# Expert rows turned by 32x32 blocks on VectorE and regrouped by SBUF transfers, from the eighth group on; last group's weight copies issued by ScalarE

## The reference

```python
H = jax.nn.gelu(xf @ W1 + b1, approximate=False)          # 128 -> 512
probs = jax.nn.softmax((H @ Wg + bg) / TEMP, axis=-1)
assign = jnp.argmax(probs, axis=-1)
for e in range(Wd.shape[0]):                               # 8 experts
    y = H @ Wd[e] + bd[e]                                  # 512 -> 128
    sel = (assign == e)[:, None]
    out = out + jnp.where(sel, probs[:, e:e + 1] * y, 0.0)
```

## Time and profile before

| | us |
|---|---|
| runs, median of 3 | 542.11 |
| lowest, highest | 538.12, 544.45 |
| the profiled execution | 537.82 |
| its span | 536.1 |

### The profile page before, as it was taken

One profiled execution on the slowest core, in us unless ns is written; L12 is line 12 of the kernel. 1 busy time (PEld: TensorE's weight loads), 2 busy tenths in 40 slices (PEclk: granted clock), 3 DMA queues, 4 the chain that ended last, 5 costly groups with the idle time before them and its releaser, 6 DMA issues.

```text
span 536.1 us, 10215 instructions
## 1 busy us (share of the span) xinstructions
PE 485.8 (91%) x3048; PEld 392.9 (73%) x3048; DVE 358.3 (67%) x1151; ACT 318.3 (59%) x572; POOL 363.9 (68%) x352
## 2 busy tenths in 40 slices
PE   8999999999999999999989777977697998997983
PEld 4788888888878888888866545645386986986972
DVE  4788777998879888888789463835554552562532
ACT  3877977688667877878795553825342333333330
POOL 4489976999879988987777754554535462564555
PEclk9999999999999999999998897978788997997998
DMA  7512454112631111111210111113212323432110
GB/s 207 151 56 86 136 168 129 46 53 58 204 94 57 54 50 52 48 49 51 60 45 29 46 45 40 40 61 107 85 34 77 89 81 109 130 121 85 50 40 21
DMA packets 66341, 42.10 MB, mean 79 GB/s; under 512 B 9436, under 2 KB 61920, under 8 KB 66288
## 3 DMA queue, kind: packets, MB, share of 16 engines
q1 hardware_dynamic: 60464, 32.13, 20.8%
q0 software_dynamic: 4224, 8.92, 4.8%
q10 hardware_dynamic: 1600, 0.40, 0.3%
HBM read 16.90 MB, written 9.84 MB: 50 GB/s over the span
## 4 chain that ended last, share of the span: by engine, by line
PE 79%; issue 6%; DVE 5%; ACT 3%; another core or an unknown queue 2%; SPq 2%; DMA 0%; POOL 0%; POOLq 0%; DVEq 0%; ACTq 0%
PE bank L594 17%; PE bank L596 17%; PE bank L595 16%; PE bank L833 12%; PE bank L625 7%; PE bank L760 2%; ACT adj_i L1043 2%; PE bank L809 1%; PE bank L716 1%; PE bank L612 1%; PE bank L632 1%; SPq L358 1%; SPq L362 1%; ACT xn L950 1%
## 5 line engine op out<-in xcount | busy, mean ns | idle before, releaser
L1043 ACT ACTIVATE adj_i<-bank,b1c 128x512 f32<-128x512 f32 x132 | 86.0, 690 | 136.8 <-PE bank L596 75.6
L559 POOL DMA_INDIRECT sorted_rows<-xrow,pos x64 | 61.9, 967 | 54.8 <-issue 54.8
L459 POOL TENSOR_TENSOR diff<-hT,n_sb 128x512 f32<-128x512 f32 x48 | 68.2, 1420 | 16.8 <-ACT n_sb L932 16.7
L833 PE MATMUL bank<-wd_sb,adj_i 128*128 x512 | 65.8, 285 | 7.4 <-issue 6.1
L833 PEld LDWEIGHTS bank<-wd_sb,adj_i 128*128 128x128 f32 x512 | 62.7, 200 | 9.4 <-issue 8.9
L594 PE MATMUL bank<-hT_hi,w_hi 128*128 128x512 f32 x132 | 61.9, 469 | 5.1 <-issue 4.0
L461 POOL TENSOR_TENSOR diff<-z_sb,diff 128x512 f32<-128x512 f32 x48 | 62.5, 1303 | 3.8
L594 PE MATMUL bank<-ag_hi,wf_hi 128*128 128x512 f32 x144 | 58.9, 409 | 0.4 <-DVE ag_lo L1198 0.3
L595 PE MATMUL bank<-hT_lo,w_hi 128*128 128x512 f32 x132 | 56.7, 430 | 2.2 <-issue 2.1
L596 PE MATMUL bank<-hT_hi,w_lo 128*128 128x512 f32 x132 | 56.8, 430 | 0.8 <-issue 0.8
L595 PE MATMUL bank<-ag_lo,wf_hi 128*128 128x512 f32 x144 | 57.0, 396 | 0.0
(11 more groups left out here) (200 smaller groups left out, 1084.8 us busy)
## 6 DMA issues: line engine op xcount, KB each, us to landing
bands<-hT SPq DMA_DIRECT2D x192, 64.0 KB, 2.2
adj_i<-sorted_rows SPq DMA_DIRECT2D x64, 72.0 KB
xrow<-in_x_dram SPq DMA_DIRECT2D x16, 256.0 KB, 3.2
adj_i<-in_adj_dram SPq DMA_DIRECT2D x16, 256.0 KB, 3.6
sorted_rows<-xrow,pos POOLq DMA_INDIRECT x64
A<-wd_sb SPq DMA_DIRECT2D x4, 256.0 KB
hT<-wd_sb SPq DMA_DIRECT2D x4, 256.0 KB
sorted_rows<-padrow SPq DMA_DIRECT2D x9, 72.0 KB
```

What stands on the lines that cost most here:

```text
L459: nc.gpsimd.tensor_tensor(diff[:, b, :], hT[:, g, :], n_sb[:, b, :], ALU.subtract).then_inc(diff_ok, 1)
L559: nc.gpsimd.indirect_dma_start(out=sorted_rows, out_offset=bass.IndirectOffsetOnAxis(ap=pos[:, g, j:j + 1], axis=0), in_=xrow[:, g * GR + ...
L833: last = nc.tensor.matmul(o, HT[:, sg % 2, k, j * P:(j + 1) * P], wd_sb[:, bass.ds(at + k * P, P)], start=(k == 0), stop=(k == KC - 1))
L1043: nc.scalar.activation(HT[:, hb, k, 0:n], HB[k][:, 0:n], ACT.Gelu, bias=b1c[:, k:k + 1]).then_inc(done, 1)
```

## The change

From group 7 on (`BANDED` = `EARLY_SG` + 1), TensorE no longer transposes the rows. VectorE normalises group s+3 in step s (it was s+2) and transposes it by 32x32 blocks into `bands` (`row_blocks`), reading every fourth element. SyncE then issues four SBUF transfers per group (`rows_turned`), which put the blocks together in `hn`, one load of rows later. ScalarE and VectorE read `hn` where they read pT. As the turned rows come in another order of columns, the Gelus undo it: `slot_gelus` reads and writes by runs of 32 elements (up to group 6 both sides are so viewed, in the same order). The copies for the last group, with their sixteen registers, go from SyncE to the end of ScalarE's steps 6 to 14. In step 4 VectorE normalises two groups, 6 and 7.

```diff
--- before.py
+++ after.py
@@ -209,6 +209,7 @@
         e_in, e_xn, e_t, e_xhi, e_xlo, e_w1, e_h, e_y, e_yb, e_yo, e_out = (
             sem("e_" + n) for n in ("in", "xn", "t", "xhi", "xlo", "w1", "h", "y", "yb", "yo", "out"))
         e_home = sem("e_home")
+        e_blk, e_col = sem("e_blk"), [sem("e_col"), sem("e_col_odd")]
         e_wd = sem("e_wd")
         e_out = [e_out] + [sem(f"e_out{n}") for n in range(1, SETS)]
         e_in = [e_in] + [sem(f"e_in{n}") for n in range(1, RING)]
@@ -319,6 +320,20 @@
         def read(sg):
 
             return 16 * sum(slots(n) * pieces(n) for n in range(sg % RING, sg + 1, RING))
+
+        BANDED = EARLY_SG + 1
+
+        def arrived(sg):
+
+            return sum(QP * 16 for k in range(BANDED, sg + 1) if k % 2 == sg % 2)
+
+        def strip(o, sg):
+
+            return o[:, 0:cols(sg)].rearrange("p (s g t) -> p s g t", s=QP, t=SUB)
+
+        def by_slot(o, sg):
+
+            return o[:, 0:cols(sg)].rearrange("p (g s t) -> p s g t", s=QP, t=SUB)
 
         def sent(n):
 
@@ -395,12 +410,14 @@
                     sp.dma_start(rows[h * n:(h + 1) * n, sg % RING, j, :],
                                  sorted_rows[bass.ds(start[k], n), :]).then_inc(e_in[sg % RING], 16)
 
-            def load_last(k, wd_at, bd_at):
-
-                j, h = divmod(k, PIECES)
-                of = slice(h * PIECE, (h + 1) * PIECE)
-                sp.dma_start(wd_last[k][:], wd_sb[:, bass.ds(wd_at[k], KC * P)]).then_inc(e_wd, 16)
-                sp.dma_start(bd_last[of, j, :], bd_bc[of, bass.ds(bd_at[k], P)]).then_inc(e_wd, 16)
+            def rows_turned(sg):
+
+                b, n = sg % 2, slots(sg) * SUB
+                sp.wait_ge(e_blk, sg - BANDED + 1)
+                hold(sp, e_xlo, sg - 1)
+                for q in range(QP):
+                    sp.dma_start(hn[:, b, q * n:(q + 1) * n],
+                                 bands[q * SUB:(q + 1) * SUB, b, 0:QP * n]).then_inc(e_col[b], 16)
 
             sp.wait_ge(tab_ok, 1)
             sp.wait_ge(g_early, EARLY * GR * 16)
@@ -420,11 +437,9 @@
             sp.wait_ge(pad_ok, (E + 1) * 16)
             for sg in range(EARLY_SG, SGROUPS):
                 load_rows(sg)
-                if sg == EARLY_SG + 2:
-                    last_at = (places(mybir.EngineType.SP, wd_tab, SGROUPS - 1, (E - 1) * KC * P),
-                               places(mybir.EngineType.SP, bd_tab, SGROUPS - 1, (E - 1) * P))
-                if inside(sg - EARLY_SG - 2, GR * PIECES):
-                    load_last(sg - EARLY_SG - 2, *last_at)
+                if sg > BANDED:
+                    rows_turned(sg - 1)
+            rows_turned(SGROUPS - 1)
             for n in range(SETS):
                 sp.wait_ge(e_out[n], sent(n) * 16)
 
@@ -852,7 +867,7 @@
                     hidden(s % 2, (2, 3), e_w1)
                     if s == SGROUPS - 2:
                         held.append(weights_at(s))
-                if inside(s + 1, SGROUPS):
+                if inside(s + 1, BANDED):
                     turned_rows(s + 1)
                 if inside(s - 1, SGROUPS):
 
@@ -1037,10 +1052,17 @@
                 act.wait_ge(g_t, g + 1)
                 nc.scalar.activation(hT_hi[:, g % 2, :], pT[:], ACT.Copy).then_inc(g_xhi, 1)
 
-            def gelus(hb, s, chunks, ready, done, n=NT):
+            def gelus(hb, s, chunks):
                 for k in chunks:
-                    hold(act, ready, s * KC + k + 1)
-                    nc.scalar.activation(HT[:, hb, k, 0:n], HB[k][:, 0:n], ACT.Gelu, bias=b1c[:, k:k + 1]).then_inc(done, 1)
+                    hold(act, g_w1, s * KC + k + 1)
+                    nc.scalar.activation(HT[:, hb, k, :], HB[k][:], ACT.Gelu, bias=b1c[:, k:k + 1]).then_inc(g_h, 1)
+
+            def slot_gelus(sg, chunks):
+                for k in chunks:
+                    hold(act, e_w1, sg * KC + k + 1)
+                    of = strip(HB[k][:], sg) if sg >= BANDED else by_slot(HB[k][:], sg)
+                    nc.scalar.activation(by_slot(HT[:, sg % 2, k, :], sg), of, ACT.Gelu,
+                                         bias=b1c[:, k:k + 1]).then_inc(e_h, 1)
 
             HB = (pR, pZ, pGH, pGI)
 
@@ -1050,11 +1072,11 @@
                 if s + 1 == GROUPS:
                     expert_high(0)
                 if s == GROUPS:
-                    gelus(0, 0, (0, 1), e_w1, e_h)
+                    slot_gelus(0, (0, 1))
                     expert_high(1)
                 if inside(s, GROUPS):
                     hold(act, g_lg, s - 1)
-                    gelus(s % 2, s, (0, 1), g_w1, g_h)
+                    gelus(s % 2, s, (0, 1))
                 if s == 0:
                     turned_high(1)
                     new_state(UN - 1)
@@ -1066,20 +1088,40 @@
                     hold(act, g_prob, s - 3)
                     nc.scalar.activation(th[:, b, :, :], sh[:, b, :, :], ACT.Tanh, scale=0.5).then_inc(g_th, 1)
                 if inside(s, GROUPS):
-                    gelus(s % 2, s, (2, 3), g_w1, g_h)
+                    gelus(s % 2, s, (2, 3))
                 if s == GROUPS:
-                    gelus(0, 0, (2, 3), e_w1, e_h)
+                    slot_gelus(0, (2, 3))
 
             def expert_high(sg):
                 n = cols(sg)
-                act.wait_ge(e_t, sg + 1)
-                nc.scalar.activation(hT_hi[:, sg % 2, 0:n], pT[:, 0:n], ACT.Copy).then_inc(e_xhi, 1)
+                if sg < BANDED:
+                    act.wait_ge(e_t, sg + 1)
+                else:
+                    act.wait_ge(e_col[sg % 2], arrived(sg))
+                of = pT[:, 0:n] if sg < BANDED else hn[:, sg % 2, 0:n]
+                nc.scalar.activation(hT_hi[:, sg % 2, 0:n], of, ACT.Copy).then_inc(e_xhi, 1)
+
+            def load_last(k, wd_at, bd_at):
+
+                j, h = divmod(k, PIECES)
+                of = slice(h * PIECE, (h + 1) * PIECE)
+                act.dma_start(wd_last[k][:], wd_sb[:, bass.ds(wd_at[k], KC * P)]).then_inc(e_wd, 16)
+                act.dma_start(bd_last[of, j, :], bd_bc[of, bass.ds(bd_at[k], P)]).then_inc(e_wd, 16)
 
             def step(s):
                 hold(act, e_y, (s - 1) * GR)
-                gelus(s % 2, s, range(KC), e_w1, e_h, cols(s))
+                slot_gelus(s, range(KC))
                 if inside(s + 1, SGROUPS):
                     expert_high(s + 1)
+                k = s - EARLY_SG
+                if k == 0:
+                    act.wait_ge(tab_ok, 2)
+                    last_at.extend((places(mybir.EngineType.Activation, wd_tab, SGROUPS - 1, (E - 1) * KC * P),
+                                    places(mybir.EngineType.Activation, bd_tab, SGROUPS - 1, (E - 1) * P)))
+                if inside(k - 1, GR * PIECES):
+                    load_last(k - 1, *last_at)
+
+            last_at = []
 
             opening()
             for s in range(FIRST_STEPS):
@@ -1513,22 +1555,35 @@
             def split_rows(sg):
                 n = cols(sg)
                 dve.wait_ge(e_xhi, sg + 1)
-                tt(hT_lo[:, sg % 2, 0:n], pT[:, 0:n], hT_hi[:, sg % 2, 0:n].bitcast(fp32), ALU.subtract).then_inc(e_xlo, 1)
+                of = pT[:, 0:n] if sg < BANDED else hn[:, sg % 2, 0:n]
+                tt(hT_lo[:, sg % 2, 0:n], of, hT_hi[:, sg % 2, 0:n].bitcast(fp32), ALU.subtract).then_inc(e_xlo, 1)
 
             def rows_normal(sg):
                 b, r = sg % 2, sg % RING
                 dve.wait_ge(e_in[r], read(sg))
-                hold(dve, e_t, sg - 1)
+                if sg - 2 < BANDED:
+                    hold(dve, e_t, sg - 1)
                 for j in range(slots(sg)):
                     ts(xn[:, b, j * P:(j + 1) * P], rows[:, r, j, 0:P], rows[:, r, j, MEAN:MEAN + 1],
                        rows[:, r, j, RSTD:RSTD + 1], ALU.subtract, ALU.mult).then_inc(e_xn, 1)
+
+            def row_blocks(sg):
+
+                b, n = sg % 2, slots(sg)
+                dve.wait_ge(e_xn, sg * GR + n)
+                hold(dve, e_col[b], arrived(sg - 2))
+                nc.vector.transpose(bands[:, b, 0:cols(sg)].rearrange("p (j g t) -> p j g t", j=QP, t=SUB),
+                                    xn[:, b, 0:cols(sg)].rearrange("p (g i j) -> p j g i", g=n, j=QP)).then_inc(e_blk, 1)
 
             def step(s):
                 fine = s - 1 >= FINE
                 if inside(s + 1, SGROUPS) and not fine:
                     split_rows(s + 1)
-                if inside(s + 2, SGROUPS):
+                if inside(s + 2, BANDED):
                     rows_normal(s + 2)
+                if inside(s + 3, SGROUPS) and s + 3 >= BANDED:
+                    rows_normal(s + 3)
+                    row_blocks(s + 3)
                 if inside(s - 1, SGROUPS):
 
                     b, r, y = (s - 1) % 2, (s - 1) % RING, (s - 1) % SETS
```

## The result

The changed kernel took 546.94 us (median of 10 runs) against 540.46 for the kernel before beside it: ratio 1.014, with a 95% interval from 1.0109 to 1.0172. (Every ratio here leaves out the runs more than 1.5% above the fastest of their kernel, so it is not quite the ratio of the two medians, 1.012.) Repeated on two other chips it was 1.0198 (1.0121 to 1.0276) and 1.0204 (1.0129 to 1.0279). Sums over this one trace are therefore set beside those of the two repeats.

What follows compares the result with a forecast made beforehand. TensorE's own work was taken to set the pace in full expert steps. Terms -4.4 + 1.3 + 0.3, and 0.3 back for steps 6 and 11, made -2.5 us: 542.1 to 539.6 us, range 532.5 to 548.5.

Steps and rivals of the forecast that it cites:

- rival B: SyncE's queue becomes the bound, its step longer than TensorE's 6.4 us: 545.5 us, 552 with a third pause; chance 0.27.
- The sum: All priced terms together for the whole kernel: -2.5 us, taking 542.1 us to 539.6.
- The removed transposes: TensorE, steps 6 to 15: ten groups lose four transposes each, 0.44 us a group, saving 4.4 us.
- rival D: Signals' lag sets the average step, so the saving only lengthens waits: steps still 6.8 us, time 542; chance 0.10.
- SyncE's queue: Four transfer issues per group, 2.5 us, make SyncE's step 6.2 us beside TensorE's 6.4; costed at 0.
- the excess: SyncE's step ran 0.8 us over its 4.9 us of work; added to the forecast 6.2 it gives 7.0 us.
- the cover: Step and a half between a transpose's blocks and their use, plus step 6's saved register loads, hides SyncE's issues: cost 0.
- Rows ahead of the outputs: VectorE, step 4: normalising groups 6 and 7 delays outputs and group 6's split; +1.3 us once, bounds 0 and 4.
- VectorE's transpose: One 32x32-block transpose of 128x512 per group, 0.70 us, bounds 0.70 to 1.4, hidden while VectorE awaits TensorE's sums.
- The Gelus: ScalarE's Gelus on runs of 32 elements: no change taken, bounds 0.57 us and twice that; well over 0.69 is wrong.
- The copies on ScalarE: Last group's copies: sixteen registers in step 6 cost 0.3 us once, between 0 and 2; later issues nothing.
- Rival C: One pause fewer in the expert steps: 533.1 us, or 536 with a shorter or later one; chance 0.25.

Runs made afterwards that it cites:

- the last kernel: Changed kernel with VectorE's rows and transpose behind the outputs, two of four SBUF transfers per group and GpSimd's second drain left out: 1.0082 of the kernel before.
- b5_both: Kernel before with the copies on ScalarE, four idle SBUF transfers a group on SyncE and rows normalised three groups ahead; TensorE turns all rows: 1.0017.
- b1_idle_copies: Kernel before with the last group's copies and registers on ScalarE, and four unused SBUF transfers a group on SyncE: 1.0045.

## Why the prediction was wrong, step by step

The forecast was 539.6 us, no change; the time was slower by more than its bound of 1%, in the direction of rival B. The sum was -2.5 us, and the loss is 6.5 us by the medians and 7.6 by the ratio. Without the credit for the transposes the sum would have been +1.6 us, so 5 to 6 us more are to be looked for in the queue and the order, priced at 0 and 1.3.

- **The removed transposes, -4.4 us: one step that failed.** The size per full step was right (6.82 to 6.38; 7.26 with eight). The credit was not. It rests on full steps setting the pace, but 40 of the 99.9 us of the stretch were pauses and the slow steps behind them, which I took as given. Taking the work away or doubling it moved the time by less than the work (1.0018 and 1.0036). That is the outcome of rival D, given 0.10, but not its mechanism: D had steps still at 6.8 us with 0.4 us idle in each, and full steps were 6.38. In the trace with one transpose, 5.5 of the 7.5 us of added idle time are the wait for group 16's rows; whether the gain goes there in other executions, or into the pauses, is not settled.
- **SyncE's queue, cost 0: the other, and the larger.** Its step was forecast at 6.2 us, 7.0 with the excess, and measures 6.35 at its quickest but 6.5 to 12.5 from loads to loads, as its register reads slow down in the pauses too. What was wrong is the cover, "the step and a half between a transpose's blocks and their use": it covers the transfers, not the row loads that queue behind them, and these were now due one step sooner. The idle transfers alone put 0.9 us of wait on the rows and the earlier rows alone 4.0; in the changed kernel, which has both, it is 21.2. Two transfers fewer take these waits away (1.7 us), at a ratio of 1.0078.
- **Rows ahead of the outputs, +1.3 us once.** The wait in step 4 (2.64 us) and the late split of group 6 (432.34, forecast 431.6, before 429.73) came as worked out; step 5 is 2.2 us longer, within the bounds of 0 to 4. "Once" was the error. With every late load the same order put the wait in front of the outputs, worst for group 16, whose eight loads take SyncE 7.06 us: 5.25 us of idle TensorE (6.7 and 5.5 in the repeats). With the rows behind the outputs the ratio was 1.0055 and 1.006.
- **Rival B** had the last loads end at 509.4 us; they ended at 510.0. That is partly luck: in the repeats it was 506.4 and 505.1. From there it went wrong: hidden layer 16 began at 531.5 us (529.3 and 527.5), not 518.7. It left out that VectorE holds the outputs while it waits for these rows.
- **VectorE's transpose** takes 1.10 us, not 0.70, inside the bounds of 0.70 to 1.4; idle, it costs nothing that matters (1.0015 with the earlier rows, on the chip without pauses).
- **The Gelus** take 0.687 us, no more than the 0.69 forecast; hT_hi from SBUF takes 0.63. Both as forecast.
- **The copies on ScalarE:** 0.9972 with the registers. As forecast, nothing.
- **Rival C**, a pause fewer: no sign of it. With one transpose there are two such steps without a named cause (11.8 and 12.0 us), as before; in the last kernel there are three (10.9 to 11.5).

What stays open: what a pause is, where the 4.4 us went, and the last 0.8% of the loss. No kernel here is shown to beat the kernel before. The nearest are the move of the copies alone, whose gain lies inside the interval, and that move with the rows earlier (ratio 1.0004, but a median of 538.70 us against 541.14).

## What to carry to other kernels

Before crediting work taken from the busiest engine, ask how much of the stretch that engine really sets: do one kernel that only leaves the work out, and see whether the time follows. An in-order queue whose own step is as long as that of the engine it feeds (6.35 and 6.38 us here) gives no cover; count what is queued behind the new issues, and by when that is due. And where an engine must wait for data of a later group, put that wait behind the work that others wait for now. And before a gap is put down to the instruction ahead of it, look for the data that the waiting one reads: in the kernel with the transfers on ScalarE the Gelu was waiting for a matmul, not for the issues in front of it.

## What the runs showed of the hardware

- The same kernel before took 475.6 us (median of 29 runs) on one chip and 540 to 545 us on all others, at granted clocks of about 0.995 and 0.95. With the idle transfers and all transposes, steps 4 to 15 took 83.3 us there (b5_both, with the rows earlier as well) and 102.5 elsewhere (b1_idle_copies).
- In a pause on the other chips TensorE's matmuls started 0.72 us apart, and a piece of SyncE's register reads took 0.70 us instead of 0.16. The cause is not known.
- VectorE's 32x32 transpose of 128x512 took 1.10 us when it read every fourth element, 0.70 us with a contiguous side (L1222). ScalarE's Gelu to and from runs of 32 elements took 687 ns, and 690 ns without them (L1043).
- On the chip without pauses the gap at a drain of GpSimd was 8.2 us behind a long row of its scatters and 3.25 us behind 24 of them.
